# A graph network with mixture-of-experts layers on one core: transposed one-hots of the attention stage made by ScalarE in two passes

## The reference

```python
h = (x @ W).reshape(n, H, C)                       # H = 4 heads, C = 64
al_src = jnp.einsum('nhc,hc->nh', h, a_src)
al_dst = jnp.einsum('nhc,hc->nh', h, a_dst)
e = jax.nn.leaky_relu(al_src[src] + al_dst[dst], 0.2)
emax = jax.ops.segment_max(e, dst, num_segments=n)
ee = jnp.exp(e - emax[dst])
denom = jax.ops.segment_sum(ee, dst, num_segments=n)
alpha = ee / (denom[dst] + 1e-16)
out = jax.ops.segment_sum(h[src] * alpha[:, :, None], dst, num_segments=n)
```

## Time and profile before

| | us |
|---|---|
| median of 3 runs | 6344.03 |
| lowest and highest | 6323.24, 6344.63 |
| profiled execution | 6309.76 |
| its span, first to last instruction | 6307.9 |

### The profile page before, as it was taken

One profiled execution on the slowest core, in us unless ns is written; L12 is line 12 of the kernel. 1 busy time (PEld: TensorE's weight loads), 2 busy tenths in 40 slices (PEclk: granted clock), 3 DMA queues, 4 the chain that ended last, 5 costly groups with the idle time before them and its releaser, 6 DMA issues. The chain is left out here.

```text
span 6307.9 us, 73562 instructions
## 1 busy us (share of the span) xinstructions
PE 4015.5 (64%) x19865; PEld 2985.1 (47%) x19865; DVE 3472.0 (55%) x9426; ACT 1590.1 (25%) x4172; POOL 3477.1 (55%) x3620
## 2 busy tenths in 40 slices
PE   5267766767667676674555655555555555555999
PEld 3145555555555555553444433444444344434666
DVE  5544444444444444443666666666666666666345
ACT  3222222222222222222122222222222222222221
POOL 3366666666666666654555655555565555652222
PEclk8578888888888888887666666666666666667999
DMA  3545444445545454442344443343444334434231
GB/s 107 179 137 142 140 139 141 141 139 141 141 138 141 139 141 138 139 127 78 111 114 115 119 116 112 112 116 111 113 120 114 106 114 115 117 110 133 73 95 41
DMA packets 338788, 767.04 MB, mean 122 GB/s; under 512 B 79991, under 2 KB 178393, under 8 KB 338239
## 3 DMA queue, kind: packets, MB, share of 16 engines
q0 software_dynamic: 202704, 594.02, 34.3%
q1 hardware_dynamic: 135662, 168.07, 8.1%
HBM read 712.95 MB, written 58.60 MB: 122 GB/s over the span
## 5 line engine op out<-in xcount | busy, mean ns | idle before, releaser
L1429 POOL DMA_INDIRECT gat_steps_rows<-table,edges x1712 | 1657.1, 968 | 1203.4 <-PE gat_steps_sum_ps L1850 488.7
L826 POOL DMA_INDIRECT flow_rows<-table,edges x1708 | 1621.8, 950 | 1063.9 <-issue 417.1
L1850 PE MATMUL gat_steps_sum_ps<-gat_steps_rows,gat_steps_onehot 128*128 128x264 f32 x3424 | 1189.9, 503 | 356.2 <-issue 288.3
L1173 PE MATMUL flow_sum_ps<-flow_rows,flow_onehot 128*128 128x256 bf16 x5124 | 837.2, 310 | 488.5 <-issue 249.0
L1850 PEld LDWEIGHTS gat_steps_sum_ps<-gat_steps_rows,gat_steps_onehot 128*128 128x128 f32 x3424 | 790.9, 245 | 595.3 <-issue 355.5
L899 DVE TENSOR_TENSOR acc<-flow_sum_ps,acc 128x256 f32 x854 | 360.5, 422 | 1132.1 <-PE flow_sum_ps L1173 570.2
L1173 PEld LDWEIGHTS flow_sum_ps<-flow_rows,flow_onehot 128*128 128x128 bf16 x5124 | 549.8, 112 | 692.6 <-issue 349.1
L1582 DVE TENSOR_TENSOR acc<-gat_steps_sum_ps,acc 128x264 f32 x856 | 369.2, 431 | 715.3 <-remote 509.7
L1225 PE MATMUL flow_y_ps<-flow_w,flow_hid 128*128 128x256 f32 x1568 | 515.5, 461 | 188.8 <-issue 118.5
L1798 PE MATMUL gat_steps_lanes_ps<-ident,gat_steps_score 128*64 128x128 f32 x214 | 73.6, 447 | 778.2 <-ACT gat_steps_score L1707 570.8
L1567 DVE TENSOR_TENSOR gat_steps_rows<-gat_steps_rows,gat_steps_weight_ps 128x1024 f32<-128x1024 f32 x428 | 505.3, 1199 | 0.5 <-issue 0.5
(11 more groups left out here) (380 smaller groups left out, 5291.0 us busy)
## 6 DMA issues: line engine op xcount, KB each, us to landing
gat_steps_drow<-drow SPq DMA_DIRECT2D x107, 512.0 KB
gat_steps_rows<-table,edges POOLq DMA_INDIRECT x1712
flow_rows<-table,edges POOLq DMA_INDIRECT x1708
expert_w<-in_L_ffn_w SPq DMA_DIRECT2D x16, 1024.0 KB
table<-start_parts SPq DMA_DIRECT2D x49, 192.0 KB, 1.8
gat_steps_mask<-masks SPq DMA_DIRECT2D x428, 12.1 KB
table<-flow_row SPq DMA_DIRECT2D x49, 130.0 KB
gat_steps_self_row<-table SPq DMA_DIRECT2D x49, 130.0 KB
```

What stands on the lines that cost most here:

```text
L826: nc.gpsimd.indirect_dma_start(out=rows[n % RING][:, t, :], out_offset=None, in_=g["table0"][:, :], in_offset=bass.IndirectOffsetOnAxis(ap ...
L1173: ins = t.matmul(sum_ps[i % 2][:, :], onehot[i // AHEAD % 2][:, i % AHEAD * T + u, :], rows[i % RING][:, u, part * D:(part + 1) * D], star ...
L1429: nc.gpsimd.indirect_dma_start(out=rows[w % RING][:, t, 0:RW], out_offset=None, in_=g["table1"][:, :], in_offset=bass.IndirectOffsetOnAxis ...
L1850: ins = t.matmul(sum_ps[(w * SPW + s) % BANKS][:, :], onehot[k][:, i, :], rows[r][:, i, :], start=(i == s * T), stop=(i == s * T + T - 1))
```

## The change

`spread_dst` moves from DVE to ACT. One comparison becomes two passes: the distance |drow - pidx| in place (Abs, with the bias -pidx, made once by DVE as `below`), then max(0, 1 - distance) (Relu, with scale -1 and bias 1). For whole numbers this is 1 where they are equal and 0 elsewhere. In program order it stands for window n + 1 behind `fades(n)` in slot w, where DVE did it for window n ahead of `scan(n)`. The second pass waits for the first by a semaphore, and for the `dst_terms` of the window before. `scan` now waits itself for the loads, as it reads the masks.

```diff
+        below = sb("below", [P, 1])
...
+        below_ready = sem("below_ready")
+        distance_ready = sem("distance_ready")
...
-            def spread_dst(w, k, trip):
-
-                dve.wait_ge(flags_in[k], trip * (16 * (H + 2)))
-                at_least(dve, dst_ready, w)
-                v.tensor_scalar(onehot_t[:, :], drow[k][:, :], g["pidx"][:, 0:1], None, ALU.is_equal).then_inc(onehot_t_ready, 1)
-
             def scan(w, k):
...
+                dve.wait_ge(flags_in[k], (w // 2 + 1) * (16 * (H + 2)))
                 dve.wait_ge(scores_turned, w + 1)
...
                 if more:
-                    spread_dst(n, k, n // 2 + 1)
                     scan(n, k)
...
+            v.tensor_scalar(below[:, :], g["pidx"][:, :], -1.0, None, ALU.mult).then_inc(below_ready, 1)
...
-            spread_dst(0, 0, 1)
...
+            def spread_dst(w, k):
+
+                act.wait_ge(flags_in[k], (w // 2 + 1) * (16 * (H + 2)))
+                s.activation(drow[k][:, :], drow[k][:, :], ACT.Abs, bias=below[:, 0:1]).then_inc(distance_ready, 1)
+                at_least(act, dst_ready, w)
+                act.wait_ge(distance_ready, w + 1)
+                s.activation(onehot_t[:, :], drow[k][:, :], ACT.Relu, bias=1.0, scale=-1.0).then_inc(onehot_t_ready, 1)
...
                     fades(n, k)
+                    if n + 1 < NW:
+                        spread_dst(n + 1, 1 - k)
                 tick(w * TICKS + 2)
 
+            act.wait_ge(below_ready, 1)
+            spread_dst(0, 0)
             pick_dst(0, 0)
             pick_dst(1, 1)
             scores(0, 0, 0, 1)
             exps(0, 0, 0)
+            spread_dst(1, 1)
             fades(0, 0)
```

## The result

| | before | after |
|---|---|---|
| median, us | 6344.33 | 6629.38 |
| lowest and highest, 4 runs each | 6323.24, 6357.65 | 6617.76, 6649.43 |
| profiled execution, us | 6309.76 | 6649.43 |

The ratio is 1.0448, with a 95% interval from 1.0418 to 1.0478: 285 us slower by the medians.

A forecast was written before the change was run, and what follows sets the result against it. No engine full; engines wait for each other in a ring, exposed at slot seams. Passes 3.95 less cover 0.83 and gain 0.1 make 3.0 us a window; 105 windows plus 4 us setup give 321, so 6665 us, range 6550 to 6795.

The forecast's parts named there:

- The removal from DVE: Taking the one-hot comparison, 792 ns a window, off DVE: worth about nothing, bounds 0 and 0.8 us a window.
- The seam: Where two attention slots meet, from ACT's fade to PE's next `turn`: PE has no work, so added ACT time delays the slot.
- Rival D: DVE sets the end of the seam: freeing it gives 1.1 us a window, 6229 us if the passes are covered; chance 0.05.
- The passes: Abs and Relu on ACT over 128x2048, behind the fade: 3.95 us a window for the pair, ends 3.5 and 4.4.
- exposed at the seam: Behind the fade, ACT's in-order passes hold up the scores, PE's `turn`, DVE's scan and POOL's next gather; forecast chance 0.73.
- the cover: ACT's idle time before three tick instructions after the fade, said to hide 0.83 us a window of the passes.
- The small gain: A longer seam lets POOL finish its gathers, bringing PE's first signals sooner: 0.1 us a window, between 0 and 0.4.
- The waits that moved: Waits for `drow`, masks and flags, and `dst_ready`, now on other engines or at other moments: said to cost nothing.
- Rival A: The seam is covered, as something not moving with `turn` sets the ring: 6344 us, from -20 to +30; chance 0.05.
- Rival B: Windows settle on a longer beat, 6791 us (chance 0.09), or a shorter one, 6480 us (chance 0.03).
- Rival C: Abs or Relu needs one or two more ACT table loads a window: 6800 to 6935 us; chance 0.05.
- PE's wait for ACT's scores: Sign in the profile after: PE's wait ahead of `turn` up from 507 by some 300 us in the same windows.

The follow-up runs named there:

- e4: Kernel before with DVE's comparison over 128 of its 2048 columns, the rest left zero: 6317.7 us, ratio 1.0015.
- e1: Changed kernel with both ACT passes ahead of the fade instead of behind it: 6329.1 us, ratio 1.0024 to the kernel before.
- e3: Changed kernel with Abs ahead of the fade and Relu behind it: 6406.7 us, ratio 1.0146 to the kernel before.
- e5: Changed kernel with both passes over 1024 of 2048 columns, the rest left zero: 5291.7 us, ratio 1.0300 to the kernel before.
- e6: Changed kernel with a second Abs pass added, values unchanged: 5671.6 us, ratio 1.1039 to the kernel before.
- e2: Changed kernel with both passes behind ACT's last tick of the slot: 6703.9 us, ratio 1.0614 to the kernel before.
- third set: Later runs on another chip, with both kernels repeated unchanged: kernel before 5148.0 us, changed kernel 5473.1 us.

## Why the prediction was right

The forecast was 6665 us, 321 more than before; the median is 6629, 285 more. The mechanism was the forecast one, and its main term came out: from the fade to the scores it takes 3.05 us more (4.46 against 1.41), where 3.95 - 0.83 = 3.12 was said. Point by point:

1. The removal from DVE was taken at nothing. The seam that was read for it can't decide this, since the comparison and `turn` both end at 4023.57 and the scan starts 0.03 us later. e4 decides: with 0.48 of the 0.79 us gone it measured no gain. Rival D, in which DVE sets the seam and the time falls to 6229, is excluded by e4 and once more by e1: there DVE is freed of all of it and ACT's passes are covered, and the time doesn't fall.
2. The passes, estimated from the shorter Relu of the expert stage at 1.99 and 1.9 to 2.0 us, took 1992 and 1909 ns, 3.90 us from the start of Abs to the next instruction (4036.33 to 4040.23); 3.95 was taken. The cost formula in the Trainium skill's "ScalarE: Activation LUTs", section "What ACT_TABLE_LOAD costs", gave 1.99 and 1.89, and the trace agrees with it within 1%.
3. That they are exposed at the seam was the step on which all rests. e1, e3, and the row of e5, the change and e6 show it: ahead of the fade 0.2%, behind it 105 times their own length less the cover.
4. The cover: 0.83 us a window were read from idle time. It fell to 0.10 in after, so 0.73 of it was used, and it came back to 0.85 in e2, which was 105 us (give or take 24) slower than the change where 87 were expected.
5. The small gain of 0.1 us from an earlier signal can't be seen. The wait for the fade grew in the profiled execution, from 5.56 to 6.18 us, while the stretch ahead of it shrank by 0.2. The medians ask for 285 / 105 = 2.7 us a window, the profiled executions for 3.5 in this stage (29.84 - 26.37), and the forecast of 3.0 lies between. The runs of after alone spread over 32 us, 0.3 us a window. On the third set's chip, where the signal is prompt, the change costs 327 us, and the forecast without this term is 332 (105 x 3.12 and the 4 us of setting up). So nothing here shows the gain, and why the first runs came out 36 us below the forecast stays open. The kernel before alone lies that far apart in two sets, 6344 and 6308 us.
6. The waits that moved cost nothing: the idle time in front of Abs, where ACT would wait for `drow`, is 0.0 us in 88 windows.

Rival A (the seam is covered) is excluded on both kinds of chip, most clearly where POOL had no gap to begin with. Rival B (a longer or shorter beat) is excluded by the even steps of e5, the change and e6 on the later chips; on the first, e3's 1.07 us for one pass speaks against it too, and so do the single windows: the short, middle and long ones (10th, 53rd and 95th of 104, from `turn` to `turn`) went from 21.8, 27.0 and 29.7 us to 24.4, 30.0 and 32.5, all by about 3 us. The prices that the prediction gave this rival don't follow from its rows: windows of 28.3 and 25.75 us against a mean of 26.5 would give 6665 + 105 x 1.8 = 6854 and 6665 - 105 x 0.75 = 6586, not 6791 and 6480. The mean granted clock of the stage, a mix of 1.2 and 2.4 GHz, fell a little, from 0.67 to 0.65, and the stretch in which PE works did not get longer (19.0 and 18.8 us). Rival C (table loads) falls by ACT's groups of after, whole span:

```profile
L1746 ACT ACT_TABLE_LOAD x97 | 124.5, 1283 | 1.7
...
L1726 ACT ACT_TABLE_LOAD x96 | 123.2, 1283 | 1.7
```

The loads in front of the exponentials are 96 as before, those at L1746 are 97 as at L1741 before, and none stands at L1703 or L1706. The Trainium skill's "ScalarE: Activation LUTs" says in "Table sets: the hidden batching unit" that relu and abs are in every set; the trace agrees.

One thing that the prediction said would be seen was sized wrongly: PE's wait for ACT's scores, "up from 507 by some 300 us in the same number of windows". It went to 873.8 us in 88 windows, which is 973 in 98. The 507 were only that part of the wait which the profile put down to ACT; it had another 197 under "issue" (704.3 us ahead of L1798 in all), and in after 873.8 of 947.1 us carry ACT's name. Taken together it is 704.3 / 98 = 7.2 us a window before and 947.1 / 88 = 10.8 after: 3.6 more, which agrees with the window. One small slip stands in its reading of the seam: PE is done not by 4014.95 us but by 4015.56, as the tick of the slot gives it two more matmuls; `turn` has 7.32 us of idle time in front. The rest came as written: ACT busy for 1988 us (2010 was said; starts that overlap by a tenth of a us twice a window make up the difference), POOL's idle time ahead of a window's gathers from 1075.8 / 98 = 11.0 to 1270.3 / 88 = 14.4 us, the window at 29.8 us (29.5 was said), ACT's wait for the fade no shorter.

## What to carry to other kernels

An idle share says nothing of what new work on an engine costs. Find the wait behind which, and the wait ahead of which, it will stand in that engine's order: here the same 3.9 us of work cost 285 us behind one wait, and 15 to 21 us ahead of it. The idle time in front of each later instruction told how much of it would be covered: the passes used 0.73 of the 0.83 us a window that were read this way. Add up a wait over all the names that the profile gives its releasers before forecasting how it will change.

## What the hardware showed that was not expected

The same kernel takes 6308 to 6344 us on some chips and 5140 to 5148 on others. In the attention stage the window is 26.4 against 20.3 us, and 5.5 of these 6.1 us are in one column of the table. That is the part inside this stage, 665 us from the first `turn` to the last (2818 against 2153). Another 496 us lie ahead of it (first `turn` at 2922.1 and at 2426.4 us), which no run here looked into. The column: from the end of PE's last matmul of the slot to ACT's fade it takes 5.56 us on the one and 0.04 on the other. The seam of the kernel before in the third set:

```profile
3520.04 0.59 PE L1842 MATMUL gat_steps_terms_ps<-gat_steps_fade_arg,gat_steps_onehot 1*128 1x4 f32 x2
...
3520.66 0.17 ACT L1727 ACTIVATE gat_steps_fade<-gat_steps_terms_ps 128x4 f32<-128x4 f32 x1 [1.81 <-PE gat_steps_terms_ps L1842]
```

In the earlier trace rows the same two are 6.1 us apart, with "remote" as the releaser; e1, on a chip of the same kind, has 7.7 us at the seam shown above, from the end of the matmul at 4033.1 to the fade at 4040.79. At the seam of the earlier trace rows DVE's add, which waits for PE too, is released with the fade:

```profile
4021.09 0.43 DVE L1582 TENSOR_TENSOR acc<-gat_steps_sum_ps,acc 128x264 f32 x1 [6.66 <-remote]
```

The prediction read there that the signal is released when POOL has run out of gathers. That holds for most slots and not for all. For windows 2 to 102 of the kernel before it is over 1 us late 90 times; in 80 of these POOL was idle when the fade started, for 2.6 us in the middle case, and in 10 it was still at its gathers. In after 69 of 89 had POOL idle. POOL itself waits for a sum of PE before its next gather, so the order doesn't tell which of the two holds the other. On the other chip the signal comes at once, though POOL goes on. The kernel with half of the gathers was meant to show whether POOL's gathers hold the signal back, but both of its runs fell on chips without the delay. So the cause stays open, and with it whether PE's matmuls end later there than the profile models them. That the delay is there before and after the change alike (5.56 and 6.18 us) is why it matters little for the cost of the change: +4.5% with it, +6.4% without.

That second ratio has two parts: the smaller base (285 / 5146 would be 5.5%), and 327 us instead of 285. The latter is 3.1 us a window, which is the pair, 3.90, less a cover of about the same size but of another make. Between 2600 and 4500 us of the kernel before in the third set, 94 windows, ACT's waits in the tick are 39.4 / 94 = 0.42 us a window, and its wait for the last gathered rows ahead of the scores adds 25.4 / 94 = 0.27:

```profile
L1707 ACT COPY gat_steps_score<-gat_steps_rows 128x64 f32<-128x64 f32 x94 | 28.3, 301 | 25.4 <-DMA gat_steps_rows<-table,edges 25.0
...
L1746 ACT ACTIVATE gat_steps_node<-gat_steps_node,gat_steps_offset,gat_steps_rstd 128x256 f32<-128x256 f32 x43 | 25.8, 599 | 6.7 <-DVE gat_steps_offset L1617 1.6
...
L1765 ACT COPY gat_steps_xn_t<-gat_steps_front_ps 128x256 f32<-128x256 f32 x43 | 16.0, 372 | 14.7 <-PE gat_steps_front_ps L1858 14.3 <-issue 0.4
...
L1752 ACT ACTIVATE gat_steps_share<-gat_steps_share 128x8 f32<-128x8 f32 x43 | 9.0, 208 | 18.0 <-DVE gat_steps_share L1593 17.6 <-issue 0.3
```

In the change on that chip all four are 0.0 in the same stretch.
